# Attention to retention: the last batch normalised inside the next stage, two roots from one variance, seven normalisations on GpSimd

## What is computed

```python
x = x + cross_attention(layernorm(x), ctx)          # 16 heads, relative bias
x = x + retnet(layernorm(x))                        # first line inside: h = rmsnorm(layernorm(x), ln1_w)
x = x + expert_layer(layernorm(x))                  # 8 experts, top 1

def layernorm(x):  m, v = mean(x), var(x);  return (x - m) / sqrt(v + 1e-5)
def rmsnorm(x, w): return x * rsqrt(mean(x * x) + 1e-6) * w
# retention: q, k, v = h @ Wq.T, h @ Wk.T, h @ Wv.T; decayed scores, group norm, gate, Wo
```

## Time and profile before

| | |
|---|---|
| median of 3 runs | 1984.2 us (1982.53 to 1984.51) |
| the profiled execution, its own time | 1984.76 us |
| its span in the trace | 1982.9 us |
| TensorE matmul busy | 1884.8 us, 95% |
| VectorE busy | 1132.3 us, 57% |
| ScalarE busy | 781.4 us, 39% |
| GpSimd busy | 803.7 us, 41% |

### The profile page before, as it was taken

One profiled execution on the slowest core, in us unless ns is written; L12 is line 12 of the kernel. 1 busy time (PEld: TensorE's weight loads), 2 busy tenths in 40 slices (PEclk: granted clock), 3 DMA queues, 4 the chain that ended last, 5 costly groups with the idle time before them and its releaser, 6 DMA issues. The chain is left out here.

```text
span 1982.9 us, 41168 instructions
## 1 busy us (share of the span) xinstructions
PE 1884.8 (95%) x17350; PEld 1443.9 (73%) x17350; DVE 1132.3 (57%) x2155; ACT 781.4 (39%) x1300; POOL 803.7 (41%) x641
## 2 busy tenths in 40 slices
PE   7999999999999999999999999779879999999995
PEld 6777777777777677677677676657657787989995
DVE  4536556656556557556556666845665353445554
ACT  3224343444444344344334333531234240455663
POOL 2116777677677667677677664000000000100001
PEclk9999999999999999999999999989889999899998
DMA  6122022122122122122121211020031202899993
GB/s 209 54 91 75 28 76 80 33 76 70 41 78 70 39 81 70 39 76 64 50 76 60 65 39 44 30 68 22 2 132 44 91 1 91 343 377 355 356 361 103
DMA packets 107817, 201.28 MB, mean 102 GB/s; under 512 B 9105, under 2 KB 46417, under 8 KB 102529
## 3 DMA queue, kind: packets, MB, share of 16 engines
q1 hardware_dynamic: 106176, 194.44, 28.9%
q0 software_dynamic: 1472, 4.40, 0.7%
HBM read 184.38 MB, written 14.44 MB: 100 GB/s over the span
## 5 line engine op out<-in xcount | busy, mean ns | idle before, releaser
L303 POOL TENSOR_TENSOR arena<-arena,probT 128x512 f32<-128x512 f32 x392 | 502.1, 1281 | 232.0 <-ACT probT L351 207.8
L456 DVE TENSOR_REDUCE negm<-bank 128x1 f32<-128x512 f32 x512 | 327.0, 686 | 181.5 <-PE bank L651 177.1
L437 DVE TENSOR_TENSOR probT<-bank,arena 128x512 f32<-128x512 f32 (+1 forms) x512 | 291.5, 616 | 212.2 <-PE bank L663 212.2
L351 ACT ACTIVATE probT<-probT 128x1024 f32<-128x1024 f32 x256 | 271.1, 1059 | 230.7 <-DVE probT L437 217.8
L345 ACT ACTIVATE arena<-bank 128x512 f32<-128x512 f32 x128 | 76.4, 597 | 474.0 <-PE bank L626 474.0
L279 POOL TENSOR_TENSOR h_lo<-ctx_raw,h_hi 128x512 fp32r<-128x512 f32 x124 | 161.0, 1299 | 172.6 <-ACT h_hi L328 168.0
L681 PEld LDWEIGHTS bank<-probT,arena 128*32 128x32 f32 x4096 | 104.0, 109 | 93.7 <-ACT probT L351 92.3
L626 PE MATMUL bank<-h_hi,w_hi 128*128 128x512 f32 x512 | 152.7, 420 | 11.2 <-ACT h_hi L328 11.2
L663 PEld LDWEIGHTS bank<-q,k 32*128 32x128 f32 x4096 | 126.0, 186 | 46.5 <-issue 44.2
L626 PE MATMUL bank<-w_hi,h_hi 128*128 128x512 f32 x512 | 152.3, 419 | 0.0
L663 PE MATMUL bank<-q,k 32*128 32x128 f32 x4096 | 150.2, 283 | 0.5 <-DVE probT L437 0.5
(11 more groups left out here) (240 smaller groups left out, 2727.3 us busy)
## 6 DMA issues: line engine op xcount, KB each, us to landing
arena<-w SPq DMA_DIRECT2D x10, 4096.0 KB, 14.5
w_sb<-w SPq DMA_DIRECT2D x40, 1024.0 KB, 6.5
x_res<-bias_table SPq DMA_DIRECT2D x64, 512.0 KB, 5.1
ctx_raw<-ctxT SPq DMA_DIRECT2D x124, 256.0 KB, 3.2
slots<-arena SPq DMA_DIRECT2D x17, 256.0 KB, 3.0
arena<-down SPq DMA_DIRECT2D x11, 256.0 KB, 2.7
b_sb<-b SPq DMA_DIRECT2D x10, 256.0 KB, 6.8
arena<-slots SPq DMA_DIRECT2D x10, 256.0 KB, 9.1
```

The source lines that it names most:

```text
L303: pool.tensor_tensor(total[:, g], total[:, g], part, ALU.add).then_inc(add_step, 1)
L351: act.activation(pT[:, u % 2, j:j + 2], pT[:, u % 2, j:j + 2], ACT.Exp).then_inc(exp_done, 1)
L437: dve.tensor_tensor(pT[:, u % 2, j, i0:], sc[:, i0:], shift[:, g, j].unsqueeze(1).broadcast_to([P, ST - i0, T]), ALU.add).then_inc(shifted, 1)
L456: dve.tensor_reduce(negm[:, c, h:h + 1], sc[:], AX.X, ALU.max, negate=True).then_inc(max_done, 1)
```

## The change

In attention, GpSimd takes the seven normalisations, from the variance alone; TensorE turns batches 0 to 3 ahead of `output(7)` and 4 to 6 behind it; everything of batch 7 but its product with wo moves into the retention block. New semaphores are shared by both blocks.

```diff
@@ attention, gpsimd, behind the loop
+                pool.wait_ge(moments, MOMENTS_DONE[0] + 2)
+                for b in range(B - 1):
+                    pool.tensor_scalar(normal[:, b, :], x_res[:, b, :], r_mv[:, b, 0:1], r_small[:, 6, b:b + 1],
+                                       ALU.subtract, ALU.mult).then_inc(normed, 1)
@@ attention, scalar
-                def root(part, first):
-                    act.wait_ge(moments, MOMENTS_DONE[first])
+                def roots():
+                    act.wait_ge(moments, MOMENTS_DONE[0])
+                    part = slice(0, B - 1)
                     act.activation(r_small[:, 0, part], r_mv[:, part, 1], ACT.Sqrt, bias=r_eps[:, 0:1]).then_inc(std_done, 1)
-                    act.wait_ge(moments, MOMENTS_DONE[first] + 3)
-                    act.activation(r_small[:, 3, part], r_small[:, 2, part], ACT.Sqrt, bias=r_eps[:, 1:2]
+                    act.activation(r_small[:, 3, part], r_mv[:, part, 1], ACT.Sqrt, bias=r_eps[:, 2:3], scale=1.0 + 1e-6
                                    ).then_inc(std_done, 1)
-                root(slice(B - 1, B), 1)
-                high_h(B - 1)
@@ attention, vector
-                scales(slice(0, B - 1), 0)
+                scales()
                 dve.wait_ge(o_mm, B * C * G)
                 dve.wait_ge(wo_mm, B - 1)
                 dve.reciprocal(aT[:], kv_bank[:].rearrange("p (g t) -> p g t", g=G)).then_inc(rinv_done, G)
                 divide(B - 1)
-                scales_end(slice(0, B - 1), 0)
                 for b in range(B - 1):
-                    normalise(b)
-                low_h(0)
...
-                low_h(B - 1)
+                    low_h(b)
@@ attention, tensor
+                for b in range(RING_BANKS - 1):
+                    turn_h(b)
                 output(B - 1)
-                for b in range(B):
+                for b in range(RING_BANKS - 1, B - 1):
                     turn_h(b)
@@ retention, scalar
+                act.wait_ge(moments, MOMENTS_DONE[1])
+                act.activation(small[:, 0, LAST:B], mv[:, LAST:B, 1], ACT.Sqrt, bias=eps[:, 0:1]).then_inc(std_done, 1)
+                act.activation(small[:, 3, LAST:B], mv[:, LAST:B, 1], ACT.Sqrt, bias=eps[:, 2:3], scale=1.0 + 1e-6
+                               ).then_inc(std_done, 1)
                 weights("rq")
+                act.wait_ge(turned, 2 * B)
+                for c in range(DC):
+                    cp = act.activation(h_hi[:, c, LAST, :], bank[6][:, c * T:(c + 1) * T], ACT.Copy, scale=ln1[:, c:c + 1])
+                cp.then_inc(h_hi_done, 1)
@@ retention, vector (last_batch: add, bn_stats, bn_aggr, two reciprocals, tensor_scalar into v; last_low: four low parts)
+                last_batch()
                 for n, job in enumerate(jobs):
                     if n == 1:
                         weights("rq")
                     if n == 3:
+                        last_low()
                         decays()
@@ retention, tensor
                 for n, job in enumerate(jobs):
+                    if n == 1:
+                        pe.wait_ge(x_done, B)
+                    if n == 3:
+                        pe.wait_ge(normed, 2 * B)
+                        for c in range(DC):
+                            mm = pe.transpose(bank[6][:, c * T:(c + 1) * T], v[:, LAST, c * P:(c + 1) * P], ident[:])
+                        mm.then_inc(turned, 1)
+                    if n == G:
+                        pe.wait_ge(h_lo_done, B)
                     project(n, *job)
```

More of the change, by code:

```diff
@@ L53 @@
 MOMENT_STEP2 = SHIFT0_FREE + 1
-MOMENT_AT = [2 * B + 3 + 2 * b for b in range(B - 1)] + [2 * B + 3 + 2 * (B - 1) + 5]
+MOMENT_AT = [2 * B + 3 + 2 * b for b in range(B - 1)] + [2 * B + 3 + 2 * (B - 1) + 2]
 MOMENTS_DONE = (MOMENT_AT[B - 2] + 1, MOMENT_AT[B - 1] + 1)
@@ L410, in _ @@
                                        ).then_inc(w_hi_done, 1)
-                root(slice(0, B - 1), 0)
+                roots()
                 for b in range(B - 1):
                     high_h(b)
-                root(slice(B - 1, B), 1)
-                high_h(B - 1)
             @block.vector
@@ L489, in moment, with scales @@
                     dve.bn_aggr(r_mv[:, b, :], stats[:, b, :]).then_inc(moments, 1)
-                def scales(part, first):
-                    n = MOMENTS_DONE[first]
-                    dve.wait_ge(std_done, 2 * first + 2)
+                def scales():
+                    part = slice(0, B - 1)
+                    dve.wait_ge(std_done, 3)
                     dve.reciprocal(r_small[:, 1, part], r_small[:, 0, part]).then_inc(moments, 1)
[L496 to L514, removed]
+                    dve.reciprocal(r_small[:, 6, part], r_small[:, 3, part]).then_inc(moments, 1)
                 def low_h(b):
@@ L531, in _ @@
                 dve.memset(r_eps[:, 1:2], 1e-6)
+                dve.memset(r_eps[:, 2:3], LN_EPS * 1e-6)
                 dve.memset(eps[:], LN_EPS).then_inc(moments, 1)
@@ L855, in retention_phase @@
         o_mm, o_out, sq_done = sem("r_o_mm"), sem("r_o_out"), sem("r_sq_done")
+        moments, std_done, normed, turned, h_hi_done, h_lo_done, wo_mm, x_in, x_done = [env[n] for n in FRONT]
+        x_row, ln1 = env["arena"][:, 16384:16896], env["ln1_sb"]
+        LAST = B - 1
         jobs = [("rk", g, f) for f in range(2) for g in range(G)] + [("rq", g, f) for f in range(2) for g in range(G)]
@@ L968, in decays, with last_batch, last_low @@
                     step(st)
+                def last_batch():
+                    dve.wait_ge(wo_mm, B)
+                    dve.wait_ge(x_in, 16 * B)
+                    dve.tensor_tensor(x_res[:, LAST, :], bank[5][:], x_row, ALU.add).then_inc(x_done, 1)
+                    dve.wait_ge(x_done, B)
+                    dve.bn_stats(pstats[:, 0, :], x_res[:, LAST, :]).then_inc(moments, 1)
+                    dve.wait_ge(moments, MOMENT_AT[LAST])
+                    dve.bn_aggr(mv[:, LAST, :], pstats[:, 0, :]).then_inc(moments, 1)
+                    dve.wait_ge(std_done, 5)
+                    dve.reciprocal(small[:, 1, LAST:B], small[:, 0, LAST:B]).then_inc(moments, 1)
+                    dve.reciprocal(small[:, 6, LAST:B], small[:, 3, LAST:B]).then_inc(moments, 1)
+                    dve.wait_ge(moments, MOMENTS_DONE[1] + 2)
+                    dve.tensor_scalar(v[:, LAST, :], x_res[:, LAST, :], mv[:, LAST, 0:1], small[:, 6, LAST:B],
+                                      ALU.subtract, ALU.mult).then_inc(normed, 1)
+                def last_low():
+                    dve.wait_ge(h_hi_done, B)
+                    for c in range(DC):
+                        lo = dve.scalar_tensor_tensor(out=h_lo[:, c, LAST, :], in0=bank[6][:, c * T:(c + 1) * T],
+                                                      scalar=ln1[:, c:c + 1], in1=h_hi[:, c, LAST, :].bitcast(F32),
+                                                      op0=ALU.mult, op1=ALU.subtract)
+                    lo.then_inc(h_lo_done, 1)
+                last_batch()
                 for n, job in enumerate(jobs):
```

33 lines of the change are left out of this document (11 added, 22 removed).

## The result

The changed kernel takes 1976.6 us (median of 7 runs, 1974.67 to 1980.21) against 1982.53 us before (7 runs): a ratio of 0.9972, 95% interval 0.9963 to 0.9981, so some 5.6 us faster. Its profiled execution took 1980.21 us, the longest of the seven, and spans 1978.4 us, 4.5 us less than the earlier trace rows.

What follows compares the result with a forecast made beforehand. It took one 23.3 us chain from attention to retention, with batch 7 as its long end, as the bound. 11.4 - 2.1 - 2.0 = 7.3 us gained, from the median of 1984.2, gave 1977.0 us; range 1972 to 1981.5.

Steps and rivals of the forecast that it cites:

- both losses behind R: After retention's first matmul (R): 2.1 us lost by the later start of decays, 2.0 us by the clock.
- the rival with 2.0 us for each normalisation: GpSimd in attention slower than its rows: retention gains 7.4 us, 3.3 overall, 1981 us; chance 0.14, shared with a hold.
- Roots and scales: Attention, ScalarE and VectorE: second root 0.26 us behind the first, long reciprocal some 0.1 us late.
- GpSimd's normalisations: GpSimd in attention: 1.0 us for each tensor_scalar, between 0.525 and 1.28, starting at about 1281.45.
- Four batches ahead of the product with wo: TensorE in attention: the product waits for batches 0 to 3 and starts later, 0.9 us lost (0 to 2.0).
- Start of retention: End of attention: retention's first matmul at 1297.5 against 1308.88, 11.4 us gained.
- Batch 7 in retention: Start of retention: VectorE finishes batch 7 in some 3.3 us, free before its copy; Wq's load covers ScalarE's roots.
- The added wait: Retention before job 5: decays starts 2.1 us later, all on the path; TensorE's stop grows to 3.2 us.
- The clock: TensorE around the stop before job 5: the clock falls, 2.0 us lost, bounds 0 and 2.9.
- the clock stays up: Rival: TensorE keeps full clock through the stops before job 0 and job 5, giving 1972.6 us; chance 0.14.
- GpSimd as the bound: Rival: GpSimd's normalisations bound attention, break-even 2.9 us each, 1992 us at 4.0 each; chance 0.05.
- met later: Rival: a stage behind waits for something that doesn't move, so the time stays within 0.2%; chance 0.05.

Runs made afterwards that it cites:

- the forms: Changed kernel with GpSimd's seven operations replaced by five kinds of operation, leaving batches 1 to 5 unnormalised; no whole time is given.
- product with wo first: Changed kernel with the product with wo ahead of all transposes, GpSimd still normalising; 1977.8 us in its only execution.
- busy stop: Changed kernel with 24 useless identity transposes on TensorE between jobs 4 and 5 of retention; 1975.6 us, ratio 0.9960 to the kernel before.
- the split: Changed kernel with the second half of decays moved from ahead of job 3's copy to ahead of job 5's; 1973.5 us, ratio 0.9959 to before.
- the last kernel: Changed kernel with VectorE normalising batches 0 to 4, GpSimd 5 and 6, product with wo last, decays split; 1969.2 us, ratio 0.9933 to before.
- GpSimd alone: Kernel before with GpSimd's seven normalisations and four batches turned ahead of the product with wo, batch 7 finished inside attention; 1977.4 us, ratio 0.9971.

## Why the prediction was right, point by point

The forecast was 1977.0 us, by 7.3 us of gain; 1976.6 and a ratio worth 5.6 us were measured. The direction was as forecast, and so were the main mechanism (batch 7 out of the chain) and both losses behind R. The term of GpSimd was wrong, and by the prediction's own signs (rows over 1.3 us) the forecast case did not happen. That the time still came within 0.4 us of the forecast is luck. In the traces the terms add up to 3.1 us, not 7.3; the profiled execution took 1980.21 us, near the 1981 of the rival with 2.0 us for each normalisation; and the forecast counted from 1984.2 us, where the seven runs of the kernel before gave 1982.53.

- *Roots and scales.* Expected the second root 0.26 us behind the first and the long reciprocal 0.1 us late. Measured 0.21 us (1280.25 to 1280.46), and the long reciprocal began 2.08 us behind the mark, against 2.14 before (1281.36 less 1279.22): not late.
- *GpSimd's normalisations.* Taken at 1.0 us, bounded by 0.525 and 1.281. Measured 2.06 us, outside the bounds that I gave the forecast. The step that failed is the placing of an operation with one input between a memset and a tensor_tensor: the forms show tensor_scalar above tensor_tensor. The rule of the Trainium skill (GPSIMD Engine Reference, Engine selection), one input at roughly line rate, fits the copy (0.61 us) and not tensor_scalar: 1.50 us and more, and 2.06 for the form that VectorE does in 3.28 / 7 = 0.47.
- *Four batches ahead of the product with wo.* Expected 0.9 us lost. The product started 11.39 instead of 6.35 us behind the mark, 5.0 us later; it then took 4.46 us to the next transposes instead of the 5.76 that the sum went by, since the clock rose earlier in it. That 1.3 us was luck of this execution: with the same code it took 5.99 us in the busy stop's. At R the order itself cost nothing that can be seen ("product with wo first").
- *Start of retention.* Expected 11.4 us earlier, measured 8.5. The rival with 2.0 us for each normalisation had priced just this at 7.4 us; the 1.3 us of the item before account for the rest. As forecast, job 0 began at the low clock (2.05 us for four matmuls).
- *Batch 7 in retention.* VectorE was done with it at 1302.68 + 0.69, 3.2 us behind R (3.3 expected), and the roots were covered.
- *The added wait.* Expected 2.1 us at `decays`; it began 13.93 instead of 11.44 us behind R, 2.5 us later. The stop before job 5 was 3.08 us (3.2 expected). In the split the stop is gone, so all of it was on the path.
- *The clock.* Expected 2.0 us, with bounds 0 and 2.9. Measured 2.9 in the changed kernel and 2.8 between the busy stop and it. So 2.9 us would have been the better price here. The row it came from the earlier trace rows doesn't warrant it: by the times from group to group that stop lost 2.6 us in the kernel before, and its equals in the other traces lost 1.6 or nothing.
- *The rivals.* That the clock stays up was wrong for both stops. "GpSimd slower than any of its rows" was right in its mechanism and gave 3.3 us; by its terms with the measured losses, 8.5 - 2.5 - 2.9 = 3.1 us. The profiled execution gained 4.5 us: the rest is 1.0 us between the scores and GLU, where the stop of 3.13 us stands in both and costs 1.1 us less of clock in the changed kernel's trace (6.64 against 7.72 us), and 0.4 us elsewhere, 0.2 of it ahead of the first mark. GpSimd as the bound didn't come: the point for it was 2.9 us each. Nothing was met later.

Why the runs gain more than the profiled pair is not settled; the executions of one kernel differ by 2 to 9 us. The mean granted clock goes along with it: the changed kernel's three longest executions (1978.1 to 1980.2 us, the profiled one among them) have 0.979, the four others (1974.7 to 1976.6 us) 0.981. What moves the clock from one execution to the next stays open.

## What to carry to other kernels

Work moved past a barrier takes its place in somebody's list there: before moving it, look for what is queued behind it on the same engine, here VectorE's decays and a copy that TensorE waits for, and move that out of the way too. Every stop of TensorE of 2 us or more before job 5 was charged twice in these traces, as waiting and as half speed behind it; that two short stops are cheaper than a long one was not tried. Price the clock as a range, since one and the same stop cost from nothing to 2.6 us of it. And before an operation goes to another engine, measure that very operation there: the dearer of the two rows that stood for it was short by a factor of 1.6, the cheaper by 3.9. Last, one trace of each kernel leaves some microseconds to the luck of the clock: compare stretches between marks, and ask the medians whether the gain is there.

## What the runs showed of the hardware that I had not expected

- On GpSimd a 128x512 fp32 tensor_scalar took 1.50 to 1.55 us with one operation and 1.93 to 2.08 us with two; tensor_tensor took 1.28, a copy 0.61.
- tensor_scalar on VectorE and on GpSimd take longer when they run at the same time. In the last kernel VectorE's five took 3.61 us (0.72 each) against 3.28 us for seven (0.47 each) with GpSimd idle, and GpSimd's two took 2.29 each against 2.06. The Trainium skill (SBUF — State Buffer, Who interferes with whom) lists VectorE's tensor_scalar among the operations that can take the port pair shared with GpSimd; the trace agrees that they interfere, at 0.2 us or so for each operation. VectorE's reciprocal and low parts, with one input from PSUM, left GpSimd's pace at 2.06 us in the changed kernel, the same as where VectorE was idle.
- Stops of TensorE of 1.07 and 1.55 us before job 5 left the granted clock at 2.4 GHz; those of 2.08, 2.19, 3.08, 3.09 and 3.11 us were followed by some microseconds at 1.2 GHz. No length parts the two cases in these traces: a stop of 2.23 us in the block behind (changed kernel, at 1488.51) and one of 3.13 us ("GpSimd alone") left it at 2.4 GHz.
